# Feature swap by transfers and new orders on three engines, with reciprocal roots by a power on GpSimd

## The reference

```python
x = L0_attn_x                                    # (16, 256, 128)
x = _layernorm(x + _L0_attn_ref(x, ...))         # a: Mamba block, four heads of 64, gated RMS norm
x = _layernorm(x + _L0_ffn_ref(x, ...))          # b: attention with a choice of 1 of 8 experts per head
x = _layernorm(x + _L1_attn_ref(x, ...))         # c: linear attention with rotary positions
x = _layernorm(x + _L1_ffn_ref(x, ...))          # d, e: soft mixture over 64 experts

def _rope(x):                                    # in block c, on q and k
    xp = x.reshape(b, n, half, 2)
    x1, x2 = (xp[..., 0], xp[..., 1])
    out = jnp.stack([x1 * cos - x2 * sin, x2 * cos + x1 * sin], axis=-1)
```

## Time and profile before

| | |
|---|---|
| median of 3 runs | 1496.24 us (1493.55 to 1498.13) |
| profiled execution | 1495.65 us, its span 1493.8 us |
| PE busy | 1434.7 us (96%) |
| DVE busy | 1205.2 us (81%) |
| ACT busy | 820.6 us (55%) |
| POOL busy | 748.6 us (50%) |
| one slot of the token part | 57.5 us |

### The profile page before, as it was taken

The page is one execution under the profiler, slowest core; times in us unless marked ns, Lnnn a source line. Parts: engine busy times, 40 slices in busy tenths (PEclk is TensorE's granted clock), DMA queues, the critical chain, the costliest instruction groups (busy, mean ns, idle before and its releaser), DMA issues. The chain is left out here.

```text
span 1493.8 us, 32591 instructions
## 1 busy us (share of the span) xinstructions
PE 1434.7 (96%) x10940; PEld 1267.7 (85%) x10940; DVE 1205.2 (81%) x2359; ACT 820.6 (55%) x1850; POOL 748.6 (50%) x1833
## 2 busy tenths in 40 slices
PE   8789999999999999999999999988999999898998
PEld 6658888888888888888888887867999999898998
DVE  6778889889888898898898887768888888757664
ACT  4354555454555464455555544306776777667775
POOL 1433346346355354454453451226777777467772
PEclk8889999999999999999999999998999999999999
DMA  5100000000000000000000004007777777887872
GB/s 194 61 8 8 1 15 2 14 16 1 15 15 2 16 5 12 15 5 12 16 1 15 8 1 128 2 3 174 196 193 193 191 192 195 264 315 297 312 304 75
DMA packets 135426, 130.43 MB, mean 87 GB/s; under 512 B 7232, under 2 KB 125248, under 8 KB 128768
## 3 DMA queue, kind: packets, MB, share of 16 engines
q1 hardware_dynamic: 135296, 128.79, 27.9%
HBM read 72.93 MB, written 55.84 MB: 86 GB/s over the span
## 5 line engine op out<-in xcount | busy, mean ns | idle before, releaser
L737 PE MATMUL ps_l<-ve_f,oe 128*128 128x128 f32 x2048 | 275.7, 279 | 0.8 <-DVE ve_f L1740 0.8
L737 PEld LDWEIGHTS ps_l<-ve_f,oe 128*128 128x128 f32 x2048 | 248.8, 192 | 23.1 <-issue 20.4
L1740 DVE SCALAR_TENSOR_TENSOR ve_f<-ps_s,oT 128x512 f32<-128x512 f32 x248 | 166.7, 681 | 4.1 <-PE ps_l L737 2.3
L2934 POOL TENSOR_TENSOR d_s<-d_ex 128x1024 f32<-128x1024 f32 x31 | 125.2, 4040 | 83.0 <-ACT d_ex L2684 82.8
L1701 DVE COPY_PREDICATED vals<-oh,ps_l 128x1024 f32<-128x1024 int32 x112 | 146.9, 1312 | 19.3 <-PE ps_l L477 17.4
L2559 PE MATMUL ps_s<-d_ex,arena 128*128 128x128 f32 x1024 | 121.1, 277 | 4.6 <-DVE d_ex L2827 4.6
L2559 PEld LDWEIGHTS ps_s<-d_ex,arena 128*128 128x128 f32 x1024 | 118.2, 194 | 5.0 <-DVE d_ex L2827 5.0
L2547 PE MATMUL ps_l<-arena 128*128 (+1 forms) x960 | 114.5, 279 | 3.9 <-ACT d_raw L2679 3.9
L1293 ACT ACTIVATE ve_f<-ps_l,r 128x128 f32<-128x128 f32 x128 | 47.3, 370 | 125.9 <-DVE r L1713 125.6
L2547 PEld LDWEIGHTS ps_l<-arena 128*128 128x128 f32 x960 | 111.9, 195 | 4.1 <-ACT d_raw L2679 4.1
L475 PE MATMUL ps_l<-veH,x1H 128*128 128x512 f32 x256 | 115.2, 450 | 0.1
(11 more groups left out here) (332 smaller groups left out, 3842.7 us busy)
## 6 DMA issues: line engine op xcount, KB each, us to landing
logits<-d_raw SPq DMA_DIRECT2D x128, 256.0 KB, 3.5
e_lt<-logits SPq DMA_DIRECT2D x32, 1024.0 KB, 5.1
y_slots<-d_ys SPq DMA_DIRECT2D x64, 256.0 KB, 4.6
d_ex<-y_slots SPq DMA_DIRECT2D x8, 1024.0 KB, 6.9
e_y<-y_slots SPq DMA_DIRECT2D x6, 1024.0 KB, 7.2
d_w<-W SPq DMA_DIRECT2D x16, 256.0 KB, 3.4
arena<-xT SPq DMA_DIRECT2D x16, 128.0 KB, 2.4
arena<-x SPq DMA_DIRECT2D x16, 128.0 KB, 2.4
```

What stands on the lines that cost most here:

```text
L737: last = pe.matmul(ps_u[:, cols], oe[:, hp, e, :], mo[:, n % MO, hp, :], start=False, stop=(e == NE - 1 and hp == HP - 1), skip_group_chec ...
L1740: V.scalar_tensor_tensor(mo[:, n % MO, :, :].rearrange("p a n -> p (a n)"), chosen_of(b, c), float(NE - e), oT[:, u, c, :, :].rearrange("p ...
L2934: G.tensor_tensor(s8[:], part[:, 0:8, :], part[:, 8:16, :], ALU.add).then_inc(n, 1)
```

## The change

1. `c_rot` is left out for batches 0 to 12. In its place SP issues two transfers from `ql` to `t1`, the odd partitions to the even ones and the reverse (64 rows of 2 KB each), when `c_q` has written `ql`. The sign moves from `rot` into `sinT`. `c_qr` then reads `t1` (SBUF) where it read PSUM, and waits for both transfers. Batches 13 to 15 keep the product.
2. PE: `b_out(t-2, 0, 2)` moves up, from behind `c_out` to ahead of `c_kv`.
3. ACT: the copy `a_yt` goes ahead of `c_kr`.
4. DVE: `b_mo(0, 0)` and `b_mo(0, 1)` go to the head of the slot, and the last tap `a_conv(t+1, 1, (3,))` goes ahead of `b_mo(1, 7)`.
5. `rsqrt` on GpSimd is two instructions: add eps, and a tensor-tensor power with a tile of -0.5. The factor 1/DI of the RMS norm goes into the scale of ACT's Square.

```diff
+def root(pool, wait_apart, done, k, source, var, eps, half, v, y):
+    wait_apart(pool, source)
+    pool.tensor_scalar(v[:], var, 1.0, eps, ALU.mult, ALU.add).then_inc(done, 1)
+    wait_apart(pool, (done, k + 1))
+    pool.tensor_tensor(y[:], v[:], half[:], ALU.pow).then_inc(done, RSQRT_OPS - 1)
...
+            def swap(b):
+                sp.wait_ge(q["c_q"], b + 1)
+                wait(sp, q["c_qr"], 2 * b)
+                sp.dma_start(t1[0:P:2, :, :], ql[1:P:2, :, :]).then_inc(q["c_swap"], 16)
+                sp.dma_start(t1[1:P:2, :, :], ql[0:P:2, :, :]).then_inc(q["c_swap"], 16)
...
                 for u in range(2):
                     load(2 * pair + u + 1, 1 - u)
+                    swap(2 * pair + u - 3)
                     store(2 * pair + u - 3)
...
-                if c:
+                if c and t - 3 >= HELD:
                     c_rot(t - 3)
...
-                dve.wait_ge(q["c_rot_ps"], b + 1)
-                V.tensor_tensor(t1[:], linear_of(b)[:].rearrange("p (a n) -> p a n", a=2),
+                dve.wait_ge(q["c_swap"], 32 * HELD + b - HELD + 1 if b >= HELD else 32 * (b + 1))
+                swapped = linear_of(b)[:].rearrange("p (a n) -> p a n", a=2) if b >= HELD else t1[:]
+                V.tensor_tensor(t1[:], swapped,
                                 sin_s[:].unsqueeze(1).to_broadcast([P, 2, L]), ALU.mult).then_inc(n, 1)
...
                 if b:
                     b_probs(t - 1, 0)
+                if a:
+                    a_yt(t)
                 if c:
                     c_kr(t - 3)
-                if a:
-                    a_yt(t)
...
-    rot[i[1::2], i[0::2]] = -1.0
+    rot[i[1::2], i[0::2]] = 1.0
     rot[i[0::2], i[1::2]] = 1.0
...
+    sinT[0::2] *= -1.0
```

More of the change, by code:

```diff
@@ L145, in token_blocks @@
         id_b = sb("id_b", [P], BF16)
+        half = sb("half", [C])
         fill = sb("fill", [L], BF16)
@@ L331, in token_blocks @@
             b_pv b_rg b_rgs b_rgb_ps b_rgb b_ot b_m_ps b_mo b_oe b_oa b_oat_ps b_x2t_ps b_x2t b_start
-            c_qk_ps c_g c_km c_q c_v_ps c_v c_rot_ps c_qr c_t2 c_krt_ps c_kr c_kv_ps c_kv c_out_ps c_z c_res c_n
+            c_qk_ps c_g c_km c_q c_v_ps c_v c_swap c_qr c_t2 c_krt_ps c_kr c_kv_ps c_kv c_out_ps c_z c_res c_n
             c_x3t_ps c_x3t c_x3""".split()
@@ L381, in rsqrt @@
             _, _, v, y, t = nbuf[n]
-            newton(pool, wait_both, norms[n]["rstd"], RSQRT_OPS * b, (source, per * b + per), var_of(n), scale, eps,
-                   v, y, t, fused)
+            if fused:
+                newton(pool, wait_both, norms[n]["rstd"], RSQRT_OPS * b, (source, per * b + per), var_of(n), scale, eps,
+                       v, y, t, fused)
+            else:
+                root(pool, wait_both, norms[n]["rstd"], RSQRT_OPS * b, (source, per * b + per), var_of(n), eps,
+                     half, v, y)
         def scale_rows(dve, n, src, dst, b):
@@ L450, in _ @@
                 load(b, b % 2)
+            swap(0)
             store(0)
@@ L457, in _ @@
             for b in range(NB - 5, HELD):
+                swap(b)
                 store(b)
@@ L779, in c_rot @@
                 pe.matmul(linear_of(b)[:, :], rot_s[:], ql[:].rearrange("p a n -> p (a n)"),
-                          start=True, stop=True, skip_group_check=True).then_inc(q["c_rot_ps"], 1)
+                          start=True, stop=True, skip_group_check=True).then_inc(q["c_swap"], 1)
             def c_krt(b):
@@ L906, in slot @@
                     b_out(t - 2, 0, 1)
+                    b_out(t - 2, 0, 2)
                 if c:
@@ L914, in slot @@
                     c_out(t - 3)
-                if o:
-                    b_out(t - 2, 0, 2)
                 if b:
@@ L1246, in a_sq @@
                         act.wait_ge(q["a_sq"], C * b + 1)
-                    nc.scalar.activation(sq[:], yg[:, c, :], ACT.Square, scale=0.5, accum_out=ssq[:, c:c + 1]
+                    nc.scalar.activation(sq[:], yg[:, c, :], ACT.Square, scale=0.5 / math.sqrt(DI), accum_out=ssq[:, c:c + 1]
                                          ).then_inc(q["a_sq"], 1)
@@ L1903, in slot @@
                 t = 2 * r + u
+                if o:
+                    b_mo(t - 2, u, 0, 0)
+                    b_mo(t - 2, u, 0, 1)
                 if b:
@@ L1909, in slot @@
                     a_xd(t)
-                if o:
-                    b_mo(t - 2, u, 0, 0)
-                if a:
                     a_xst(t)
                     a_gm(t)
-                if o:
-                    b_mo(t - 2, u, 0, 1)
                 if b:
@@ L2014, in slot @@
                     b_rg(t - 1, 3)
+                if more:
+                    a_conv(t + 1, 1, (3,))
                 if o:
@@ L2017, in slot @@
                 if more:
-                    a_conv(t + 1, 1, (3,))
                     a_xbc(t + 1)
@@ L2199, in _ @@
             G = nc.gpsimd
+            G.memset(half[:], -0.5)
             def a_am(b):
```

## The result

The change made the kernel slower: 1507.71 us median of 4 executions (1506.85 to 1509.1), against 1496.1 us for the kernel before on the same chip; the ratio is 1.0082 with a 95% interval of 1.0069 to 1.0095. The profiled execution took 1509.1 us, its span 1507.4 us.

What follows compares the result with a forecast made beforehand. PE and DVE bound the kernel as two carriers of one loop. Twelve slots 1.09 us longer give +13.1, less 3.1 ahead of them: +10.0 on 1495.65, median 0.6 above, 1506.2 us; 8 in 10 range 1487 to 1516.

Steps and rivals of the forecast that it cites:

- One sign that I had named as showing me wrong: At c_qr on DVE: the prediction would be wrong if c_qr waits for a transfer.
- What bounds: Slot as a loop of PE and DVE: a_op hands to DVE, last mask hands back with 0.95 us to spare.
- The rotation: Product removed from PE: at most 0.85 us a slot, 0.6 lost waiting at a_yt; c_krt moves by only 0.2 us.
- The transfers: SP's two transfers from ql to t1: 1.7 us to landing, so hidden with 1.7 us to spare.
- my far end of 4.6: Slowest landing time taken for the transfers, from a 256 KB store in small pieces; qr then 1.2 us later.
- The rival of late transfers: Transfers land 4.6 us after issue, 1.2 us late, on top of the rest: about 1519 us; chance 0.08.
- `b_out(0, 2)` and the copies: Before c_kv on PE, yT first on ACT: a_op and DVE's a_res 0.50 us later, PE 0.40 us ahead.
- The roots: GpSimd's roots lose 12 of 14 instructions; with a 0.2 us power, b_vg starts at about 529.6 instead of 534.02.
- Where `b_vg` lands: Beside c_qr and taps on DVE: two products hold it 0.8 us each, a_res 1.17 us later; the deciding term.
- The estimate of 0.2 us more: Collision of b_vg with DVE by the page's full block, 1.02 us per product: about 0.2 us a slot dearer.
- The masks and the tap: End of DVE's stretch: tap takes 0.87 of 0.95 us to spare, leaving 0.08; early masks give nothing.
- Ahead of the slots: Before PE's first q and k product: short root of ln2, batch 0, gives back 3.1 us (1.5 to 6).

Runs made afterwards that it cites:

- e3_power_alone: Kernel before with part 5 alone, the power in every root of GpSimd that is not fused; slots 58.60 us, 1503.4 us, ratio 1.0058.
- e8_reordered: e6_swap_alone with an exponential run early on ACT, a_yt ahead of c_kr, and two b_out moved up on PE; slots 57.23 us, 1489.71 us, ratio 0.996.
- e10_max_first: e8_reordered with DVE's maximum b_max(1) moved ahead of the mask b_mo(0, 6); slots 56.82 us, 1483.33 us, ratio 0.9912.
- e6_swap_alone: e4_power_vg_late with part 1 of the change, transfers in place of the product, old orders; slots 57.52 us, 1492.89 us, ratio 0.9981.
- e1_vg_late: Whole change, with GpSimd's b_vg also waiting until DVE has written kv; slots 57.90 us, 1500.31 us, ratio 1.0028 to the kernel before.
- e7_orders_alone: e4_power_vg_late with parts 2 to 4 of the change and the sign in the sine, product still on PE; slots 57.90 us, 1497.9 us, ratio 1.0016.
- e4_power_vg_late: Kernel before with the power roots and b_vg waiting for DVE's kv; slots 57.51 us, 1489.76 us, ratio 0.9955.

## Why the prediction was right, and where not

The forecast was 1506.2 us, slower; measured are 1507.71 us. The mechanism was right, but that the sum came so near is in part luck, by errors that offset each other: the forecast of +10.0 us had the pieces -3.1 and +13.1, the profile has -4.4, +10.6 in the slots of the usual length, 6.2 for late transfers, and about 1 for the rest. One sign that I had named as showing me wrong did appear: `c_qr` waits for a transfer, in 2 of 13 slots.

- **What bounds.** PE and DVE as two carriers of one loop was the right picture, and the last mask is one place where DVE hands back: it ends 0.06 us ahead of the last `b_out` in the change, as in the four other kernels that have the tap ahead of the mask, and in no kernel that has it behind. What I missed is that DVE hands back earlier as well. In the change 0.62 us of the 0.88 are already on PE behind `b_turn`, half a slot earlier, where DVE's maximum lets ACT make the softmax and PE turn it; the last 0.1 us come at the mask. Since the two places ask nearly the same of PE, no run tells which of them would carry the change alone. Where the mask has room, the earlier places count alone: `kv` at `c_out` in `e3_power_alone`, and `b_turn` in `e8_reordered`, where an exchange of two DVE operations (`e10_max_first`) gave 0.41 us a slot.
- **The rotation.** Right, and more than said. That the copy ending just ahead of `a_yt` would hold PE is in the row as 0.56 us (0.6 was said). I gave the steady slot nothing for the product, and `e6_swap_alone` gives exactly nothing. What I did not name was the work that makes `kr` late on ACT, the table load of 1.28 us ahead of the softmax; `e8_reordered` moves it, and the softmax starts 4.63 us behind `km` where it was 6.11.
- **The transfers.** Near the end that I took: 2.0 us to landing in the median (1.7 was said), and hidden in 11 of 13 slots. What was wrong is that I took one value for all slots. Twice the second transfer was late, with 4.0 and 2.9 us, within my far end of 4.6, and this cost 6.2 us with what followed; 3.4 of them are the lower clock, which no other run with the transfers shows. There the slot of batch 2 is only 0.2 to 1.3 us longer than its neighbours. The rival of late transfers was made for all slots at once; as two single cases it had its place in the sum.
- **`b_out(0, 2)` and the copies.** 0.50 us later at `a_op` was said, 0.46 us is measured (`e1_vg_late`), and its price is paid by DVE as described. `e7_orders_alone` has the price of all orders, 0.39 us a slot.
- **The roots.** The direction was right, the size not. A power takes 0.69 to 0.77 us, not 0.2, and `b_vg` starts 1.39 us after the root began (0.9 was said). It spared the first operation of `c_qr`, and hit the second and the tap.
- **Where `b_vg` lands.** Right: 0.8 us twice was said, 1.50 - 0.69 = 0.81 and 1.66 - 0.87 = 0.79 are measured. `a_res` was to be 1.17 us later; it is 10.04 - 9.10 = 0.94 us later, counted from `km`. `e3_power_alone` shows that this alone costs 1.07 us a slot, and `e4_power_vg_late` that nothing else in the roots does. The estimate of 0.2 us more that I made by the Trainium skill (page SBUF — State Buffer, section Who interferes with whom) was too low by its own terms: two holds of 1.02 us in place of 0.8 add 0.44 us to DVE's own work, so that `a_res` would start at 536.08, 0.34 us later than the 535.74 of the sum.
- **The masks and the tap.** The tap ahead of the last mask was said to use 0.87 of the 0.95 us to spare, and this to close the loop. It did: the mask ends 1.69 us later than before, 0.94 from `a_res` and 0.75 from the tap, and 0.06 us are left of the 0.95. The forecast of 1.09 us a slot (0.88 measured) is too high mainly by `a_res`, 1.17 said and 0.94 measured. In `e1_vg_late`, where PE is only 0.24 us late behind `b_turn`, the mask adds the last 0.13 us.
- **Ahead of the slots.** 3.1 us was said, from the root of batch 0. There the power takes 1.48 us, since it stands beside a DVE operation with two SBUF inputs, the layer norm follows at 52.31 where it was 55.67, and the first `km` is 4.4 us earlier. Of these 4.4 us some 1.7 go with the granted clock, which was low for 27.3 us ahead of it and not for 30.7. In the eleven kernels with the power the first `km` stands at 173.0 to 179.3 us, in the two with the Newton steps at 180.3 and 181.7: the gain is real, but 4.4 is the value of one pair of executions.

## What to carry to other kernels

A shorter operation can make a kernel slower, even on an engine with time to spare (the short roots alone cost 1.07 us a slot): ask of each what stands behind it in its queue, and what that will then run beside. An instruction taken off a full engine gives nothing while the engine comes early to an operand that another engine delivers at a fixed time; find that deliverer, move its work, and only then count the saving. And when a delay is expected to be handed on, look at every operation of the late engine that another one reads, not only at the last one in the loop.

## What the runs showed of the hardware

- **Two SBUF inputs on DVE beside a GpSimd product.** How long DVE is held depends on how far the product has come. Started 0.08 us after the product, a 0.69 us operation takes 1.50 us (held 0.81). At 0.38 us (`e3_power_alone`) it takes 1.21 us (held 0.52), at 0.57 us (the slot of batch 2) 1.02 us (held 0.34), and at 0.68 us (t = 15) 0.91 us (held 0.23). The sum of offset and hold is 0.89 to 0.91 us, a little less than a product's 1.02 us. The Trainium skill, page SBUF — State Buffer, section Who interferes with whom, says that a DVE instruction with two SBUF inputs contends with a GpSimd instruction that reads SBUF, that the shared ports are an exclusive lock, and that the order of issue decides who blocks; these four rows agree to 0.13 us, and they replace the flat 0.8 to 1.0 us with which I worked. Size does not protect: 128x4 values took 0.78 us. The products are stretched as well, from 2.04 to 2.49 us for two.
- **A power on GpSimd.** 128x2 values take 0.69 us, 0.77 for the root of the RMS norm, against 0.20 us for most of the Newton instructions. One took 1.48 us (50.79, the root of `ln2` of batch 0), beside a DVE operation with two SBUF inputs that had started at 50.51 and took 1.22 us: the block works in this direction too.
- **The table load.** From its start to that of the first exponential it takes 1.30 us (530.28 to 531.58) in the kernel before and 1.29 us (522.62 to 523.91) in its new place in `e8_reordered`. The Trainium skill, page ScalarE: Activation LUTs, section What ACT_TABLE_LOAD costs, gives about 1283 ns for the load and about 1380 ns more for a drain. The load agrees. No drain is seen: in the kernel before, the copy ahead of the load ends at 530.26, 0.02 us before it starts.
- **The clock after an idle PE.** After waits of 0.56 and 2.15 us within 3 us the granted clock was 0.83 in the next 10 us. After 0.56 and 1.01 us at the same place (`e6_swap_alone`) it stayed at 1.00. At t = 15 it was 0.90 from 880.6 to 890 with a wait of 2.67 us in the change, and 1.00 after a wait of 2.22 us in `e6_swap_alone`. The late transfer of batch 2 thus cost 3.1 us in the one kernel and 0.84 in the other, in part by the clock (1.7 us) and in part by the longer wait.
- **Late transfers.** In the change and in all five experiments with the transfers, DVE waited for those of batches 2 and 12, and for no others. Of the 78 pairs in these six traces 21 have a packet of the queues that load instructions between the first issue and the second landing, and in each of them the second transfer took 2.3 to 4.0 us; in the other 57 it took 2.0 or 2.1 us. This goes together without exception, but that the packets are the cause was not tested.
